# Two-layer cross-attention on one core: the blocks between a unit's five score runs dealt out anew, with a bank and an engine named for each

## The chip, the cores and the metric

The kernel runs on one core of a Trainium2 chip. The time is the device time of one launch in microseconds (us); smaller is better. The engines are TensorE (PE, with its weight loads as PEld), VectorE (DVE), ScalarE (ACT), GpSimd (POOL) and SyncE (SP), which here issues every DMA. Each engine works through its own list of instructions in order, and a semaphore wait at the head of a list holds everything behind it.

## The reference

Two layers of cross-attention over 32 sequences of 256 tokens (width 320, 20 heads of 16), each against 77 text rows of width 512. Cut to what matters, both layers are:

```python
q = heads(x @ Wq)                       # 20 heads of width 16
k, v = heads(text @ Wk), heads(text @ Wv)
p = softmax(q @ k^T / 4)                # over the 77 text rows
x = x + (merge(p @ v) @ Wo + bias)      # layer 1 reads layer 0's x
```

The further text parts of the reference (object, others, ip) have no rows for this input.

## The kernel before

The 8192 tokens are cut into 16 chunks of 512 (two sequences each); the two layers give 32 **units** u. Every fp32 product is made of rounded parts: a value's high part and what is left over (names ending in `S` hold both; `KH`/`KL`, `QH`/`QL`), with three products of high and low parts in place of one, 12 matrix instructions for a block of K or V (4 slices of the 512 inputs), 8 for a block of 128 outputs of Q or O, and 5 for the last 64 outputs.

Everything is written out by hand, engine by engine. One unit u on PE is:

- five **runs** `run(u, k, n)`: the scores of group k of unit u against the keys (24 products into the four banks of `pA`, then 16 more that subtract each row's maximum), and woven into them 8 products of unit n = u+1 in tokens-by-keys order, into two pairs of banks of `pR`. They serve only to find the maxima (`X` on DVE, a `tensor_reduce`). The first pair is written at the run's start (steps 0 and 1), the second at its end (steps 10 and 11).
- after each run ACT takes the exponential of all four banks of `pA` (`S`, the line of `ACT.Exp`); the next run writes `pA` and so waits for it (`take_four`). What PE does between two runs is called a **gap** here; a pair of an even and an odd unit has ten.
- in the gaps stand the other **blocks**: `K(w, m)` and `V(w, t)` of the next pair of units w (three each), `Q(u+2, m)` (three a unit), `PV(u, k)` (five a unit: probabilities times values, with the sums), `out(z, m)` of unit z = u-2 (three a unit, called O below), and `max_rows`, the transposition of the maxima, copied to `Mt` by ACT before the next unit's first run.

Every block takes one bank of `pR`, which is free again when DVE or ACT has read it. Before, the four banks go round in turn (`take`), and the reductions of the first pair of maxima free their two banks together.

From PV to O a unit goes a long way: DVE or ACT copy the five results to `Oraw` (`o_copy`); SP moves the sums to `Zg` and `Zt` (`sums`), DVE inverts them (`recip`), SP writes them to DRAM (`put_recips`) and reads them back spread over rows (`spread`, into `OS`); SP moves the rest of `Oraw` to `On` in 12 transfers (`natural`); POOL multiplies (`normalise`), ACT rounds and POOL and DVE take what is left over (`split_o`), then PE can run O. SP also loads the values into `VA` (`values`, three transfers a unit), stores the result of unit z (`store`) and loads X for unit u+3 (`load_x`) into one of five buffers, the one that unit z has just left. `split_x` on ACT and POOL makes the rounded parts of X.

Two of the waits that the text below speaks of, as the code has them before and after:

```python
if k == 0 and u:                       # o_copy, before it overwrites Oraw
    dve.wait_ge(d_on, 128 * u)         # all of natural(u-1, 0) and (u-1, 1) landed
    dve.wait_ge(d_zg, 32 * u)
...
if u >= XR:                            # load_x on SP
    sp.wait_ge(d_y[x], 32 * (u // XR)) # the store from this buffer landed
```

Of the kernel before, what the change touches and what calls it, by code (L numbers as in the profile page):

```python
# [47 lines left out]
def build(nc, a):  # L48
    with ExitStack() as ctx:
# [3 lines left out]
        def sem(name):  # L53
# [4 lines left out]
        Wk = sb("Wk", [128, 2, 4, KC], F32R)  # L58
# [10 lines left out]
        KH = sb("KH", [128, 3, 3, 2, LK], F32R)  # L69
        KL = sb("KL", [128, 3, 3, 2, LK], F32R)  # L70
# [13 lines left out]
        Zt = sb("Zt", [32, 64])  # L84
        stage = sb("stage", [128, 4, KC])
# [5 lines left out]
        ones = sb("ones", [L, 2, 2 * D])  # L91
# [9 lines left out]
        w_hi, x_hi, v_copied, q_hi0, q_hi1, q_hi2, q_half, mt_copied, p_done, o_hi = (  # L101
            sem(f"s_{n}") for n in (
                "w_hi", "x_hi", "v_copied", "q_hi0", "q_hi1", "q_hi2", "q_half", "mt_copied", "p_done", "o_hi"))

        w_lo, q_lo0, q_lo1, q_lo2, q_summed, x_max, r_done, r_last, o_tail, y_done, neg_done = (
            sem(f"s_{n}") for n in ("w_lo", "q_lo0", "q_lo1", "q_lo2", "q_summed", "x_max", "r_done", "r_last",
                                    "o_tail", "y_done",
                                    "neg_done"))
# [5 lines left out]
        o_raw = [sem(f"s_o_raw{k}") for k in range(NG)]  # L114
# [26 lines left out]
        VN = stage[:, :, :].rearrange("p k c -> p (k c)")[:, 0:4 * C].rearrange("p (t x) -> p t x", t=2)  # L141
        OL = stage[:, :, :].rearrange("p k c -> p (k c)").rearrange("p (m n) -> p m n", m=3)
        RL = C32[:, :, :].rearrange("p k n -> p (k n)")

        def k_parts(w):

            first = 2 * w % 3
            if first < 2:
                return [(slice(first, first + 2), slice(0, 4))]
            return [(slice(2, 3), slice(0, 2)), (slice(0, 1), slice(2, 4))]  # L150
# [11 lines left out]
        def _(pe):  # L162
            ring = [None] * NR
            turn = 0
            four = None

            def take(key, *readers):

                nonlocal turn
                b = turn % NR  # L170
# [228 lines left out]
            for m in range(3):  # L399
                K(0, m)  # L400
# [775 lines left out]
```

## Time and profile before

| what | us |
|---|---|
| three runs | 1049.4, 1052.84, 1042.22 (median 1049.4) |
| the profiled execution | 1039.82 |
| its span, first to last instruction | 1038.0 |
| PE / DVE / ACT / POOL busy | 936.3 / 638.4 / 553.8 / 385.5 |

The profiled execution lies 1.78 us above its span and 0.9% below the median of the three. Its sixteen pairs of units start at 43.31, 106.71, 170.49, 231.41, ..., 968.18 us; in between, most take 60.9 or 61.0 us, some 61.9 to 63.8. A pair starts with the first run of its even unit. In the timeline matrix instructions overlap, so what a block costs is read from its start to the start of what follows, not from its duration.

### The profile page before, as it was taken

What the parts mean: (1) busy time and instruction counts of PE and PEld (TensorE: products, weight loads), DVE (VectorE), ACT (ScalarE), POOL (GpSimd) and SP (SyncE); (2) the same over time, 40 slices, a digit from 0 to 9 for tenths busy, and PEclk for the clock granted to TensorE, in tenths of its full rate; (3) what the DMA queues carried; (4) which work ended last, traced back from release to release, by engine and by line L of the source; (5) the groups of instructions that cost most, each with busy time, mean ns of one, the idle gap of its engine ahead of it and who ended that gap; (6) DMA issues with size and microseconds to landing.
All of it is one profiled execution on the core that took longest, in us unless ns stands there. A gap on an engine that the chain in (4) does not pass through costs nothing.

```text
span 1038.0 us, 30058 instructions
## 1 busy us (share of the span) xinstructions
PE 936.3 (90%) x12848; PEld 741.2 (71%) x12848; DVE 638.4 (61%) x1007; ACT 553.8 (53%) x598; POOL 385.5 (37%) x208
## 2 busy tenths in 40 slices
PE   5799999999898999989999999999999999998987
PEld 5577767777676777777677777767777776876755
DVE  5554656666666566666656666665666656666636
ACT  4445545555555565556655654565554555555532
POOL 3403425334233523526453542533333252342023
PEclk9787989999999999999999999999999999999978
DMA  7203334443434364343535334353443434433232
GB/s 236 71 13 80 84 100 104 134 115 109 112 85 119 105 170 110 107 112 94 161 105 158 104 90 126 82 137 109 126 118 86 107 99 134 114 103 90 70 96 70
DMA packets 81491, 112.80 MB, mean 109 GB/s; under 512 B 22160, under 2 KB 38838, under 8 KB 81360
## 3 DMA queue, kind: packets, MB, share of 16 engines
q1 hardware_dynamic: 81360, 110.88, 39.3%
q8 instruction: 103, 1.69, 0.7%
q14 instruction: 28, 0.23, 0.1%
HBM read 60.50 MB, written 22.24 MB: 80 GB/s over the span
## 4 chain that ended last, share of the span: by engine, by line
PE 63%; DVE 22%; issue 6%; ACT 5%; DMA 2%; SPq 1%; POOL 1%; ACTq 0%; POOLq 0%; DVEq 0%
PE pR L239 29%; PE pR L212 9%; PE pR L226 9%; PE pR L348 8%; DVE Mx L720 7%; DVE X L786 4%; PE pA L293 4%; DVE KL L685 4%; PE pR L284 3%; DVE QL L694 2%; DMA OS<-rd 2%; PE pA L299 2%; ACT KH L507 2%; DVE Oraw L735 1%; DVE KH L679 1%
## 5 line engine op out<-in xcount | busy, mean ns | idle before, releaser
L566 ACT ACTIVATE P<-pA 77x2048 f32<-77x2048 f32 x160 | 300.2, 1876 | 261.1 <-PE pA L299 261.0
L720 DVE TENSOR_REDUCE Mx<-pR 128x8 f32<-128x616 f32 x320 | 247.4, 795 | 61.0 <-PE pR L284 60.2
L911 POOL TENSOR_TENSOR On<-On,OS 128x1024 f32<-128x1024 f32 (+1 forms) x62 | 112.7, 1837 | 340.0 <-DMA OS<-rd 340.0
L348 PE MATMUL pR<-P,VA 77*32 77x256 f32 x2480 | 165.6, 399 | 32.3 <-DVE Mx L720 32.0
L239 PE MATMUL pR<-XS,Wq 128*128 128x512 f32 x672 | 173.7, 402 | 2.6 <-DVE Mx L720 2.5
L284 PE MATMUL pR<-KH,QH 32*128 32x154 f32 x1280 | 141.8, 298 | 37.9 <-DVE Qt L702 15.6
L284 PEld LDWEIGHTS pR<-KH,QH 32*128 32x128 f32 x1280 | 102.0, 191 | 94.5 <-issue 72.9
L239 PE MATMUL pR<-OS,Wo 128*128 128x512 f32 x630 | 164.4, 409 | 4.9 <-DVE Mx L720 4.9
L293 PE MATMUL pA<-QH,KH 32*77 32x256 f32 x1280 | 150.1, 299 | 3.7 <-ACT Mt L556 3.6
L881 POOL TENSOR_TENSOR XS<-X,XS 128x1024 fp32r<-128x1024 f32 x32 | 76.4, 2386 | 197.6 <-ACT XS L495 197.6
L348 PEld LDWEIGHTS pR<-P,VA 77*32 77x32 f32 x2480 | 95.0, 142 | 76.3 <-issue 53.7
L239 PEld LDWEIGHTS pR<-OS,Wo 128*128 128x128 f32 x630 | 115.7, 191 | 44.7 <-issue 12.6
L239 PEld LDWEIGHTS pR<-XS,Wq 128*128 128x128 f32 x672 | 122.4, 190 | 30.7 <-DVE Mx L720 4.8
L293 PE MATMUL pA<-QL,KH 32*77 32x256 f32 x1280 | 140.0, 282 | 0.0
L293 PE MATMUL pA<-QH,KL 32*77 32x256 f32 x1280 | 139.9, 282 | 0.0
L735 DVE COPY Oraw<-pR 128x512 f32<-128x512 f32 x123 | 84.5, 687 | 40.9 <-PE pR L348 40.9
L212 PE MATMUL pR<-CS,Wk 128*128 128x308 f32 x576 | 95.8, 318 | 14.2 <-DVE Wk L661 10.6
L299 PE MATMUL pA<-Mt,neg 32*77 32x128 f32 x2560 | 106.8, 229 | 0.0
L694 DVE TENSOR_TENSOR QL<-pR,QH 128x512 fp32r<-128x512 f32 x64 | 44.2, 691 | 101.1 <-ACT QH L514 101.0
L786 DVE SCALAR_TENSOR_TENSOR X<-pR,bias,X 128x512 f32<-128x512 f32 (+1 forms) x93 | 69.3, 745 | 55.9 <-PE pR L239 55.9
L299 PEld LDWEIGHTS pA<-Mt,neg 32*77 32x77 f32 x2560 | 102.6, 147 | 0.0
L212 PEld LDWEIGHTS pR<-CS,Wk 128*128 128x128 f32 x576 | 87.3, 197 | 18.5 <-issue 15.9
(81 smaller groups left out, 1181.3 us busy)
## 6 DMA issues: line engine op xcount, KB each, us to landing
On<-Oraw SPq DMA_DIRECT2D x248, 64.0 KB
OS<-rd SPq DMA_DIRECT2D x62, 256.0 KB
C<-in_cT SPq DMA_DIRECT2D x16, 616.0 KB, 4.8
X<-in_xT SPq DMA_DIRECT2D x16, 512.0 KB, 3.9
y<-X SPq DMA_DIRECT2D x16, 512.0 KB, 4.0
X<-y SPq DMA_DIRECT2D x16, 512.0 KB, 3.9
out<-X SPq DMA_DIRECT2D x15, 512.0 KB, 4.0
X<-in_xT SPq DMA_DIRECT2D x32, 128.0 KB, 4.1
```

The costliest lines, as they stand in the source:

```text
L212: f = pe.matmul(p[:, 0:L4], Wk[:, s, k, 128 * m:128 * m + 128], CS[:, c, k, :], start=(k == 0 and s == 0 and c == 0), stop=(k == 3 and s = ...
L226: f = pe.matmul(out, CS[:, c, k, 128 * t:128 * t + M], Wv[:, s, k, :], start=(k == 0 and i == 0), stop=(k == 3 and i == 2))
L239: f = pe.matmul(p[:, :], W[:, k, c0:c0 + 128], S[:, s, :], start=(i == 0), stop=(i == len(pairs) - 1))
L284: return pe.matmul(pR[:, pair + j % 2, t * LK:t * LK + LK], QH[32 * j:32 * j + 32, n % 2, c0:c0 + 128], KH[32 * j:32 * j + 32, m, n % 3, b ...
L293: pe.matmul(pA[0:L, j, h * SQ:h * SQ + SQ], K_[32 * j:32 * j + 32, ms, u % 3, bs, pp * L:pp * L + L], Q_[32 * j:32 * j + 32, u % 2, c0:c0 ...
L299: return pe.matmul(pA[0:L, j, t * 128:t * 128 + 128], neg[32 * j:32 * j + 32, i:i + 1].broadcast_to([32, L]), Mt[32 * j:32 * j + 32, :], s ...
L348: f = pe.matmul(bank[32 * j:32 * j + 32, b * SQ:b * SQ + SQ], VA[0:L, u % 2, b, h:2 * C:H], src, start=True, stop=True, skip_group_check=True)
L566: act.activation(P[0:L, i % PR, :, :], pA[0:L, :, :], ACT.Exp, scale=float(D) ** -0.5).then_inc(p_done, 1)
L720: dve.tensor_reduce(Mx[:, :].rearrange("p (j i) -> p j i", j=4)[:, 2 * half:2 * half + 2, i:i + 4], pR[:, pair:pair + 2, 0:2 * LK].rearran ...
L735: dve.tensor_copy(Oraw[:, k, :], pR[:, slot["PV", u, k], :]).then_inc(o_raw[k], 1)
L786: dve.scalar_tensor_tensor(out=X32[0:M, x, m, :], in0=p[0:M, :], scalar=bias[0:M, l, m:m + 1], in1=X32[0:M, x, m, :], op0=ALU.add, op1=ALU ...
L911: pool.tensor_tensor(On[rows, blocks, :], On[rows, blocks, :], OS[rows, blocks, :].bitcast(F32), ALU.mult).then_inc(o_mul, 1)
```

## The change

- The bank is no longer taken in turn: each block's call names its bank, and each run names its first and second pair. In the prologue, and in the last unit, blocks also use the four banks of `pA`.
- The blocks of a pair of units are dealt over its ten gaps in a new order. DVE and ACT each get new lists: all copies of V are on DVE, eight of ten `o_copy` on ACT (before two), some roundings of Q and K on DVE (`Q_hi`, `K_hi`). SP's and POOL's lists are rewritten to fit.
- The maxima of a run's first pair of banks are two reductions, one for each bank (`X(n, k, part)`), each with its own semaphore; the second pair stays one reduction.
- The last block of K (64 outputs) takes 8 matrix instructions in place of 12: its 128 columns hold the high part's 64 and the left-over part's 64 side by side, and the two halves are added afterwards (`k_half_copy` on ACT, `k_sum` on DVE) into `Kt`. `KH2`/`KL2` hold this block, 2x77 wide for two sequences instead of 4x77.
- `Wk` is loaded 320 wide instead of 384.

The core of the diff:

```diff
-                p = take(("K", w, m), (k_lo[m], w + 1))
-                for k in range(4):
-                    for s, c in ((0, 0), (0, 1), (1, 0)):
+                if m == 2:
+                    p = take(("K", w, m), bank, (k_summed, w + 1))
+                    for k in range(4):
+                        pe.matmul(p[:, 0:L4], Wk[:, k, 256:384], CS[:, 0, k, :], start=(k == 0), stop=(k == 3), ...)
+                    for k in range(4):
+                        f = pe.matmul(p[0:64, 0:L4], Wk[:, k, 256:320], CS[:, 1, k, :], start=False, stop=(k == 3), ...)
...
+    # PE, one unit in full
+                if u % 2 == 0:
+                    run(u, 0, n, 2, 0)
+                    V(w, 2, 2)
+                    K(w, 1, 3)
+                    Q(u + 1, 1, 1)
+                    out(z, 1, 0)
+                    run(u, 1, n, 2, 0)
+                    out(z, 0, 3)
+                    V(w, 1, 1)
+                    run(u, 2, n, 2, 0)
+                    out(z, 2, 2)
+                    Q(u + 2, 2, 3)
+                    K(w, 2, 0)
+                    PV(u, 0, 1)
+                    run(u, 3, n, 2, 0)
+                    Q(u + 2, 0, 2)
+                    PV(u, 1, 3)
+                    run(u, 4, n, 0, 2)
+                    Q(u + 2, 1, 1)
+                    max_rows(n, 3)
+                    V(w, 0, 0)
+                    PV(u, 2, 3)
+                    PV(u, 4, 1)
+                    PV(u, 3, 0)
+                else:
+                    run(u, 0, n, 2, 0)
+                    out(z, 0, 2)
+                    run(u, 1, n, 0, 2)
+                    out(z, 1, 0)
+                    run(u, 2, n, 2, 0)
+                    PV(u, 0, 3)
+                    PV(u, 1, 0)
+                    run(u, 3, n, 2, 0)
+                    out(z, 2, 2)
+                    Q(u + 2, 2, 0)
+                    PV(u, 2, 1)
+                    run(u, 4, n, 2, 0)
+                    K(w + 1, 0, 2)
+                    max_rows(n, 1)
+                    Q(u + 2, 0, 3)
+                    PV(u, 4, 1)
+                    PV(u, 3, 0)
...
+    # ACT, even unit, behind its fifth run
+                    S(u, 4)
+                    max_rows(n)
+                    split_o(v, 0)
+                    split_x(u + 3)
+                    split_o(v, 1)
+                    o_copy(u, 4)
+                    o_copy(u, 3)
...
+    # SP, even unit
+                    sums(v, 2)
+                    values(u + 1)
+                    sums(v, 1)
+                    put_recips(v, 1)
+                    put_recips(v, 0)
+                    for r in range(3):
+                        natural(v, r)
+                    spread(v, 0)
+                    spread(v, 1)
+                    store(z)
+                    load_x(u + 3)
+                    load_c(u // 2 + 2)
+                    sums(u, 0)
...
+    # SP, odd unit
+                    sums(v, 2)
+                    sums(v, 1)
+                    if u < NU - 1:
+                        values(u + 1)
+                    natural(v, 0)
+                    put_recips(v, 0)
+                    put_recips(v, 1)
+                    natural(v, 1)
+                    natural(v, 2)
+                    spread(v, 0)
+                    spread(v, 1)
+                    store(z)
+                    if u < NU - 1:
+                        sums(u, 0)
+                    load_x(u + 3)
```

Here v = u-1, z = u-2 and w = u//2 + 1. Each place below is given as the engine's list has it, before and after.

PE, the first gap of an even unit, from the end of the run to the start of the next. Before (`L348` PV, `L239` O):

```order
L299 MATMUL pA<-Mt,neg 77x128 x2
L284 MATMUL pR<-KH,QH 128x154 x2
L348 MATMUL pR<-P,VA 32x256 x16
L239 MATMUL pR<-OS,Wo 128x512 x8
L284 MATMUL pR<-KH,QH 128x154 x2
```

Now (`L253` V, `L237` K, `L266` Q and O):

```order
L340 MATMUL pA<-Mt,neg 77x128 x2
L321 MATMUL pR<-KH,QH 128x154 x2
L253 MATMUL pR<-Wv,CS 52x320 x12
L237 MATMUL pR<-CS,Wk 128x308 x12
L266 MATMUL pR<-XS,Wq 128x512 x8
L266 MATMUL pR<-OS,Wo 128x512 x8
L321 MATMUL pR<-KH,QH 128x154 x2
```

Two PVs have moved to the end of the unit ahead; V, K, Q and another block of O stand here instead, 44 block products in place of 24.

SP, an odd unit, from the sums to the spread. Before (`L1013`, `L1018` the sums, `L1030` and `L1036` natural, `L1043`, `L1046` the inverted sums to DRAM, `L1060` spread):

```order
L1013 DMA Zg<-Oraw 64x1x64
L1018 DMA Zt<-Oraw 32x1x64
L1030 DMA On<-Oraw 16x2x512 x4
L1043 DMA rd<-Zg 128x64
L1046 DMA rd<-Zt 32x64
L1036 DMA On<-Oraw 16x512 x4
L1060 DMA OS<-rd 128x1x512 x2
```

Now (`small` holds what `Zt` held; `L1182` is `values`):

```order
L1200 DMA small<-Oraw 32x1x64
L1195 DMA Zg<-Oraw 64x1x64
L1182 DMA VA<-VS 77x320
L1182 DMA VA<-VS 51x320
L1182 DMA VA<-VS 26x320
L1212 DMA On<-Oraw 16x2x512 x4
L1226 DMA rd<-Zg 128x64
L1229 DMA rd<-small 32x64
L1212 DMA On<-Oraw 16x2x512 x4
L1219 DMA On<-Oraw 16x512 x4
L1243 DMA OS<-rd 128x1x512 x2
```

The first four natural transfers of a unit used to be issued ahead of this place, in the unit before; now they stand here, behind the three of the values.

DVE, an odd unit, from the inverted sums to the maxima of the fourth run. Before (`L741`, `L747` recip, `L786`, `L790` O, `L720` maxima, `L735` o_copy):

```order
L741 RECIPROCAL Zg<-Zg 128x64
L747 RECIPROCAL Zt<-Zt 32x64
L786 SCALAR_TENSOR_TENSOR X<-pR,bias,X 64x512
L790 TENSOR_TENSOR X<-pR,X 64x512
L786 SCALAR_TENSOR_TENSOR X<-pR,bias,X 128x512
L720 TENSOR_REDUCE Mx<-pR 128x2x4 x2
L735 COPY Oraw<-pR 128x512 x2
L720 TENSOR_REDUCE Mx<-pR 128x2x4 x2
```

Now (`L887`, `L893` recip, `L931` O, `L866` maxima, `L881` o_copy):

```order
L887 RECIPROCAL Zg<-Zg 128x64
L893 RECIPROCAL small<-small 32x64
L931 SCALAR_TENSOR_TENSOR X<-pR,bias,X 128x512
L866 TENSOR_REDUCE Mx<-pR 128x4 x2
L866 TENSOR_REDUCE Mx<-pR 128x2x4
L881 COPY Oraw<-pR 128x512
L866 TENSOR_REDUCE Mx<-pR 128x4 x2
L866 TENSOR_REDUCE Mx<-pR 128x2x4
```

One of the two o_copy has gone to ACT; the other, o_copy(u, 0), still stands between the maxima of runs 2 and 3, and waits for `d_on`.

## Rows read from the trace of the kernel before

**Rows 1.** Page, part 1: busy us, share of the span, instructions of each engine.

```profile
PE 936.3 (90%) x12848; PEld 741.2 (71%) x12848; DVE 638.4 (61%) x1007; ACT 553.8 (53%) x598; POOL 385.5 (37%) x208
```

**Rows 2.** Windows: stretch, length, busy us (count) PE PEld DVE ACT POOL, clock, DMA share, GB/s.

```profile
43.31:106.71 63.40, 54.49 (x725) 43.50 (x724) 32.19 (x58) 33.04 (x37) 13.23 (x7) 0.78 0.17 41
477.57:538.55 60.98, 56.34 (x800) 44.79 (x800) 38.56 (x60) 35.81 (x38) 28.80 (x15) 1.00 0.46 128
968.18:1038.00 69.82, 57.56 (x798) 41.41 (x797) 38.73 (x46) 25.83 (x24) 14.38 (x8) 0.85 0.30 84
```

**Rows 3.** Timeline of PE: start, duration, instruction, count, idle time before.

```profile
408.87 3.23 PE L239 MATMUL pR<-XS,Wq 128*128 128x512 f32 x13
...
411.96 3.73 PE L226 MATMUL pR<-Wv,CS 128*128 128x320 f32 x24
415.63 0.34 PE L284 MATMUL pR<-KH,QH 32*128 32x154 f32 x2
...
418.20 1.96 PE L348 MATMUL pR<-P,VA 77*32 77x256 f32 x32 [1.14 <-DVE Mx L720]
...
462.77 0.34 PE L284 MATMUL pR<-KH,QH 32*128 32x154 f32 x2
...
464.13 1.96 PE L212 MATMUL pR<-CS,Wk 128*128 128x308 f32 x12
465.93 2.00 PE L239 MATMUL pR<-XS,Wq 128*128 128x512 f32 x8
```

**Rows 4.** Waits: who waited for whom, total us, times, longest.

```profile
PE pR L348 <- DVE Mx L720: 32.0, 42, 1.1
```

**Rows 5.** DVE by shape: line, names, shapes, count, busy us, mean ns, idle before.

```profile
L720 DVE TENSOR_REDUCE Mx<-pR 128x8 f32<-128x616 f32 x320 | 247.4, 795 | 61.0 <-PE pR L284 60.2
...
L685 DVE SCALAR_TENSOR_TENSOR KL<-pR,mask,KH 128x308 fp32r<-128x308 f32 x66 | 32.5, 534 | 31.8 <-ACT KH L507 31.3
...
L685 DVE SCALAR_TENSOR_TENSOR KL<-pR,mask,KH 128x154 fp32r<-128x154 f32 x60 | 18.5, 371 | 19.9 <-ACT KH L507 19.7
```

**Rows 6.** Timeline of ACT behind the run that starts at 415.63.

```profile
417.09 1.87 ACT L566 ACTIVATE P<-pA 77x2048 f32<-77x2048 f32 x1 [0.62 <-PE pA L299]
```

**Rows 7.** ACT by shape: rounding X, and one copy of a result (columns as in rows 5).

```profile
L495 ACT ACTIVATE XS<-X 128x1536 fp32r<-128x1536 f32 x32 | 47.2, 1476 | 1.1 <-DMA X<-in_xT 1.1
...
L574 ACT ACTIVATE Oraw<-pR 128x512 f32<-128x512 f32 x32 | 19.0, 597 | 26.1 <-PE pR L348 26.1
```

**Rows 8.** Timeline of SP: start and duration of the issue (not of the transfer).

```profile
420.13 0.63 SPq L1013 DMA_DIRECT2D Zg<-Oraw  x1
...
421.64 2.64 SPq L1030 DMA_DIRECT2D On<-Oraw  x4
424.96 0.34 SPq L1043 DMA_DIRECT2D rd<-Zg  x1
...
428.39 1.91 SPq L1060 DMA_DIRECT2D OS<-rd  x3
...
430.83 0.53 SPq L1071 DMA_DIRECT2D y<-X  x1
437.52 0.38 SPq L970 DMA_DIRECT2D X<-in_xT  x1
437.94 1.14 SPq L972 DMA_DIRECT2D X<-in_xT  x2
439.18 2.48 SPq L1000 DMA_DIRECT2D VA<-VS  x3
```

**Rows 9.** Timeline of POOL: the product released by the spread issued at 428.39.

```profile
434.14 3.64 POOL L911 TENSOR_TENSOR On<-On,OS 128x1024 f32<-128x1024 f32 x2 [9.97 <-DMA OS<-rd]
```

**Rows 10.** DMA issues, KB each, median us from issue to landing.

```profile
On<-Oraw SPq DMA_DIRECT2D x124, 32.0 KB, 1.9
...
y<-X SPq DMA_DIRECT2D x16, 128.0 KB, 6.5
```

**Rows 11.** Line 972 (X for a later unit), issue to landing.

```profile
DMA to landing us min/median/max: 3.7/4.0/8.2
```

More of the change, by code:

```diff
@@ L196, in take_four @@
                     pe.wait_ge(four[0], four[1])
+                else:
+                    for b in range(NR, 2 * NR):
+                        for reader in ring[b] or ():
+                            pe.wait_ge(*reader)
                 four = (freed, value)
+                for b in range(NR, 2 * NR):
+                    ring[b] = (four,)
             def weights(name, l):
@@ L401, in _ @@
-            for m in range(3):
-                Q(0, m)
-            for t in range(3):
-                V(0, t)
-            for k in range(NG):
-                run(None, k, 0)
-            Q(1, 0)
-            max_rows(0)
-            Q(1, 1)
-            Q(1, 2)
+                pe.wait_ge(o_tail, u + 1)
+                pe.wait_ge(o_lo, u + 1)
+                p = take(("O", u, m), bank, freed)
+                project(p, Wo, OS, m).then_inc(o_pe, 1)
+            K(0, 0, 4)
+            K(0, 1, 5)
@@ L650, in _ @@
+            for k in range(NG):
+                S(NU - 1, k)
+            split_o(NU - 2, 0)
+            split_o(NU - 2, 1)
             for m in range(3):
@@ L847, in _ @@
-            o_copy(v, 4)
+                    maxima(n, 0, 0, 1, 2)
+                    recip_last(v)
+                    recip(v)
+                    split_o(z)
+                    K_lo(w, 1)
+                    V(w, 2)
+                    Q_lo(u + 1, 1)
+                    out(z, 1)
+                    maxima(n, 1, 1, 0, 2)
+                    out(z, 0)
+                    V(w, 1)
+                    maxima(n, 2, 0, 1, 2)
+                    out(z, 2)
+                    q_sum(u + 2)
@@ new lines, in _ @@
+                    k_sum(w)
+                    maxima(n, 3, 0, 1)
+                    K_hi(w, 2)
+                    maxima(n, 3, 2)
+                    K_lo(w, 2)
+                    Q_lo(u + 2, 0)
+                    maxima(n, 4, 1, 0, 2)
+                    Q_hi(u + 2, 2)
+                    Q_lo(u + 2, 2)
+                    Q_hi(u + 2, 1)
+                    Q_lo(u + 2, 1)
+                    V(w, 0)
+                    o_copy(u, 2)
+                    split_o(v)
+                else:
+                    maxima(n, 0, 0, 1, 2)
+                    out(z, 0)
+                    maxima(n, 1, 0, 1, 2)
+                    recip(v)
+                    recip_last(v)
+                    out(z, 1)
+                    maxima(n, 2, 1, 0, 2)
+                    o_copy(u, 0)
+                    maxima(n, 3, 0, 1, 2)
+                    out(z, 2)
+                    q_sum(u + 2)
+                    maxima(n, 4, 0, 1, 2)
+                    Q_hi(u + 2, 2)
+                    Q_lo(u + 2, 2)
+                    K_hi(w + 1, 0)
+                    K_lo(w + 1, 0)
+                    Q_lo(u + 2, 0)
@@ L848, in _ @@
+            u, v, z = NU - 1, NU - 2, NU - 3
             out(z, 0)
+            out(z, 1)
             recip(v)
@@ L984, in values @@
                 w, half = u // 2, u % 2
-                sp.wait_ge(v_copied, 3 * w + 2 + half)
+                for t in (half, half + 1):
+                    sp.wait_ge(v_copied[t], w + 1)
                 if u == NU - 1:
```

850 lines of the change are left out of this document (445 added, 405 removed).

## The prediction

> **What bounds the kernel now.** I read the busy times first: PE is busy 90% of the span, no other engine above 61% [rows 1]. Then the windows: a pair of units in the middle takes 60.98 us at full clock, the first pair 63.40 at 0.78, though it has no O blocks, the end 69.82 at 0.85 [rows 2]. So the kernel is sixteen equal laps, and a lap is worth reading block by block on PE's timeline [rows 3]. A run is 1.36 us to its successor (462.77 to 464.13), a K block 1.80 (464.13 to 465.93), 13 products of Q 3.09 (408.87 to 411.96), two V 3.67 (411.96 to 415.63), two PVs 1.96. A lap of ten runs (13.6), three K (5.4), three V (5.5), 42 products of Q and 42 of O (84 at 0.24 = 20.2), ten PVs (9.6) and two transpositions (0.2) comes to 54.5. The other 6.4 us of 60.9 are waits of PE, mostly for a bank: 1.14 before a PV, until DVE has reduced the run's last maxima; in all 32.0 us in 42 such waits [rows 3, 4].
>
> **The change part by part.** *K's third block:* four products fewer a lap, each 1.80/12 = 0.15: -0.6 a lap, -9.6 in all 16, all on PE's path. What it adds (a copy on ACT, sums on DVE) has a gap to hide in.
>
> *The new deal.* A bank is named so that the first block of a gap goes to one whose maxima are long reduced. In the even unit I find no block that needs the bank of the second pair before DVE is through with it, so the 6.4 us can go. But a gap has a floor: the exponential starts 1.46 us behind the run's start and takes 1.87 [rows 3, 6], so runs are at least 3.4 apart. In the odd unit the gaps 0 to 2 hold one O, one O and two PVs, 1.8 to 2.0 us, just at that floor: +0.5 a lap with the last maxima before PV(u, 1). The even unit is then five runs, 6.8, and gaps of 7.4, 3.9, 4.5, 2.9 and 6.8 = 32.3 us by the blocks above, the odd, from run to run, 3.4, 3.4, 3.5, 4.8, 7.2 = 22.3: a lap of 54.6 (54.5-0.6+0.5 says the same within 0.2).
>
> *The split maxima.* 308 elements are not in the trace as a reduction. The products of K with 154 and 308 elements take 371 and 534 ns, 1.06 ns an element, so half of the 795 ns reduction is 795-326 = 469, and two are 0.14 us more than one [rows 5]: 160 times, 23 us of DVE work. Bounds: 0 (nothing but the elements) and 0.4 each (no saving by size). With eight copies on ACT, DVE's 38.6 us in a lap [rows 2] become about 40; the extra hides behind PE, except where DVE's list is held.
>
> *SP's list: where the gain is given back.* An issue costs SP time: a sum 0.63, four natural 2.64, an inverse 0.34, three values 2.48, the spread 1.91, X 1.52 [rows 8]. And load_x(u+3) waits until store(z) has landed, 6.5 us behind its issue [rows 10]: 430.83 to 437.52 SP does nothing [rows 8]. The replay, from an even unit's start:
> - SP comes out of the last load_x at +1.2. Sums 2 to 1.8, values to 4.4, sums 1 to 5.0, landed about 6.3 (1.9 from issue, as a natural transfer [rows 10]). recip stands on DVE ahead of split_o(z), so that ends near 7.6, and O(z, 1), due at 6.9, starts at 7.7: **+0.8**.
> - O(z, 2) ends at 17.6; spread must wait for it: 17.7 to 19.6; the second store at 20.1, landed 26.6; X issued to 28.1, landed 31.5 (4.0 [rows 11]). ACT stands before split_x(u+3) from 30.0 on: 1.5 for it, then about 0.6 for split_o's small half and twice 0.6 for the copies [rows 7], 34.9. The next unit starts at 33.3 and needs the second copy's bank at its eleventh step of twelve, 34.4: **+0.5**.
> - Odd unit, from its start: o_copy(v, 3) done 1.7, sums to 2.4, values to 4.9, natural(v, 0) to 7.5, both inverses to 8.3, natural(v, 1) to 10.9, landed 12.2. DVE's o_copy(u, 0) waits for that landing, and run 3 waits for its bank: 12.9 in place of 10.6: **+2.3**. Behind the waiting copy on DVE stand the maxima of run 3; PE has nothing in between.
> - O(z, 2) ends 15.7, spread to 17.6, store landed 24.6, X issued to 26.1; the unit ends at 25.0, which gives the +1.2 above back: the lap closes on itself.
>
> A lap: 54.6+0.8+0.5+2.3 = 58.2. The spread has room: POOL starts 5.75 behind its issue and needs 3.64 [rows 8, 9], done at 27.1 and 25.4 where ACT comes at 29 and 25.7.
>
> On this the Trainium skill speaks otherwise: "DMA: Bandwidth & Descriptors", section "Issuing engines are not separate DMA queues", calls the sequencer's time to initiate a DMA "usually small relative to the DMA itself". By it the three waits would shrink to the first two rivals' side. Rows 8 show 0.6 of issue against 1.9 of landing for a natural transfer, so here the issues count.
>
> *Prologue.* K(1, 0) is added to it and Q(1, 1) leaves it; run 0 now also waits for K(1, 0)'s left-over on DVE, since that block sits in a bank of `pA`. DVE gets that block's four 0.53 us operations and five split maxima [rows 5]. I take the first run at 45.1, 1.8 later than 43.31 [rows 2] (bounds -3 and +4: the V blocks between the maxima may win more).
>
> *First lap.* No O and no store wait: about 51.3 at full clock. Before, the same sum is 60.9-10.2 = 50.7 and it took 63.40 with the granted clock at 0.78 [rows 2], so the slow clock cost 12.7. Here gaps are as empty; I take 9.7 (bounds 0 and 13): 61.0. The Trainium skill, "TensorE: Matmul & The Clock Gate", section "What's actually happening", says that the throttled state is the default and activity releases it; a busier first lap would then come to the lower end, 51.3.
>
> *End.* The last unit's new list uses `pA` banks, but split_o(30) on DVE now stands behind three divisions; against that ACT copies the maxima earlier in its list. The laps' two SP waits stand there too. 68 in place of 69.8 (bounds 61 and 72).
>
> **Sum.** 45.1 + 61.0 + 14 x (58.2 + 0.5) + 68 = 996; the 0.5 is what the laps before average above 60.9. With 1.8 around the span, 998 against 1039.8; the median is 0.9% above that execution, so **1007 us**, -4%.
>
> **The rivals.**
> - *A, the deal works as dealt.* The three SP waits don't bite (earlier issues or quicker transfers): laps of 54.6+0.5, first lap 57, end 63: 45+57+771+63+2 = 938, times 1.009 = **946**. For it: every term of 54.6 is a measured block. Against: the issues are measured too. In between, with the +2.3 alone gone, 970.
> - *B, only K's products count.* The waits move and don't go, since DVE's list has an operation in every gap that PE needs: 1049.4-9.6 = **1040**. DVE at 40 of 58 us makes it possible, the named banks speak against it.
> - *C, slower.* X for unit u+3 is now needed right after it lands, in the even unit. If it lands like the slowest, 8.2 us instead of 4.0 [rows 11], each lap is 4.2 longer: 62.4, in all 1055 times 1.009 = **1064**. It decides from 2.7 us a lap on. Against it: the median is 4.0, and DMA is busy under half of the time [rows 2].
>
> **Chances.** A change of 1% is about what can be told. Forecast 0.72 (own range 962 to 1035), A 0.13, B 0.07, C 0.06, rest 0.02. Faster by over 1% (below 1038.9) takes the forecast and A: 0.86; same 0.08; slower 0.06. The range reaches into A and to B, 946 to 1040, and leaves out C and A's lower half.
>
> **What would show it.** Laps of 58.2, the longest PE wait in an odd unit before run 3, released by `Oraw` on DVE, itself held by the landing of `On`; a wait before O(z, 1) in the even unit; ACT idle for X before split_x; no waits of PV for `Mx`. A is right if laps are 55 and PE idles only 0.1 before runs. I am wrong if `Mx` still ends PE's waits, or if the clock falls inside the middle laps.

## The result: 1075.2 us, 2.6% slower, and the profile after

The change makes the kernel slower: 1075.24 us (median of 1072.38, 1073.21, 1077.26 and 1080.05) against 1049.12 on the same chip, a ratio of 1.026 with a 95% interval of 1.019 to 1.033. The prediction said 1007, 946 to 1040. The profiled execution took 1072.38 with a span of 1070.6, so some 1.8 us around the span are as before.

The page of the kernel after, parts 1 and 4 (busy time, and the chain that ended last by engine and line):

```profile
PE 946.5 (88%) x12784; PEld 745.4 (70%) x12784; DVE 652.6 (61%) x1190; ACT 554.4 (52%) x564; POOL 389.5 (36%) x209
...
PE 53%; DMA 20%; SPq 12%; issue 7%; DVE 5%; ACT 3%; DVEq 0%; ACTq 0%
PE pR L266 22%; PE pR L387 7%; DMA out<-X 7%; PE pA L334 7%; DMA y<-X 6%; PE pR L321 6%; DMA Zg<-Oraw 5%; PE pR L253 4%; SPq L1243 4%; SPq L1182 3%; PE pA L340 3%; SPq L1153 2%; PE pA L266 1%; ACT Oraw L659 1%; DVE Mx L866 1%
```

Nearly a third of the chain is now transfers and SP's issues: the store (`out<-X`, `y<-X`), the sums (`Zg<-Oraw`), the spread (`L1243`), the values (`L1182`), the loads of X (`L1153`). PE has 64 instructions fewer than in [rows 1] (four for each of sixteen K blocks) and is busy for 10 us more: some of its instructions ran at the lower clock (the granted clock is 0.94 in the mean, before 0.97).

Windows of the first lap, one in the middle, and the end (columns as in rows 2):

```profile
45.13:108.71 63.58, 56.72 (x752) 44.32 (x752) 31.05 (x62) 30.58 (x29) 14.83 (x8) 0.76 0.17 39
745.92:809.34 63.42, 58.00 (x798) 46.02 (x794) 39.78 (x74) 33.91 (x34) 23.33 (x13) 0.95 0.41 108
996.95:1070.60 73.65, 56.07 (x777) 40.92 (x773) 40.43 (x48) 28.69 (x26) 18.86 (x11) 0.88 0.31 80
```

A lap in the middle is 63.4 us where it was 60.98 at full clock [rows 2]. From the starts of the even units on PE's timeline, the fourteen middle laps are 63.45 us in the mean against 61.53 before. That is where the loss comes from: first run +1.8, first lap +0.2, 14 laps x 1.92 = +26.9, end +3.8; in all 32.7 us, which are, but for rounding, the 32.6 between the two profiled executions.

The waits of PE and of those that it waits for (waiter <- releaser: us in total, times, longest):

```profile
PE pR L321 <- DVE Oraw L881: 46.4, 15, 4.4
...
ACT Oraw L659 <- DMA On<-Oraw: 37.7, 14, 3.8
...
DVE Zg L887 <- DMA Zg<-Oraw: 19.4, 15, 2.4
PE pR L266 <- DVE OS L922: 19.3, 13, 2.6
...
ACT XS L549 <- DMA X<-y: 16.5, 8, 2.7
...
PE pR L266 <- DVE Mx L866: 10.6, 11, 1.7
```

The 32.0 us in which PV waited for `Mx` [rows 4] are gone: for PV the named banks do what they were named for. In their place stand, thirteen to fifteen times each, a wait of up to 4.4 us for `o_copy` and one for `split_o`. ACT waits for X in both layers, 16.5 us in eight laps of the second and 13.1 us in seven of the first. Waits for `Mx` remain before blocks of Q and O, 10.6 us in 11; nine of them stand before O(z, 0) of an odd unit, and a fence below shows why.

The lap that starts at 745.92, on PE's timeline (columns as in rows 3):

```profile
754.32 2.11 PE L266 MATMUL pR<-OS,Wo 128*128 128x512 f32 x8 [1.54 <-DVE OS L922]
...
765.28 0.73 PE L226 MATMUL pR<-CS,Wk 128*128 128x308 f32 x4
765.85 0.72 PE L229 MATMUL pR<-CS,Wk 128*64 128x308 f32 x4
766.50 1.10 PE L387 MATMUL pR<-P,VA 77*32 77x256 f32 x16
...
781.64 0.34 PE L321 MATMUL pR<-KH,QH 32*128 32x154 f32 x2 [0.25 <-ACT Oraw L659]
...
788.84 2.19 PE L387 MATMUL pR<-P,VA 77*32 77x256 f32 x32
794.67 0.49 PE L321 MATMUL pR<-KH,QH 32*128 32x154 f32 x2 [3.63 <-DVE Oraw L881]
```

In order: O(z, 1) of the even unit waits for `split_o`; the 8-product block of K takes 1.22 us (765.28 to 766.50); the odd unit's run 0 is held at its last steps; run 3 of the odd unit waits 3.6 us for the bank that `o_copy(u, 0)` reads. The releasers, on DVE and on ACT, first DVE:

```profile
751.08 0.55 DVE L893 RECIPROCAL small<-small 32x64 f32<-32x64 f32 x1 [2.78 <-DMA small<-Oraw]
752.99 0.55 DVE L887 RECIPROCAL Zg<-Zg 128x64 f32<-128x64 f32 x1 [1.37 <-DMA Zg<-Oraw]
753.58 0.68 DVE L922 TENSOR_TENSOR OS<-On,OS 64x512 fp32r<-64x512 f32 x1
...
793.83 0.69 DVE L881 COPY Oraw<-pR 128x512 f32<-128x512 f32 x1 [4.04 <-issue]
```

```profile
778.62 1.49 ACT L549 ACTIVATE XS<-X 128x1536 fp32r<-128x1536 f32 x1 [1.77 <-DMA X<-y]
780.01 0.62 ACT L667 ACTIVATE OS<-On 64x512 fp32r<-64x512 f32 x1
780.53 1.06 ACT L659 ACTIVATE Oraw<-pR 128x512 f32<-128x512 f32 x2
```

In another lap, of the first layer, the same late rounding holds PE a second time. DVE's `split_o` waits for ACT's rounding of O, which stands behind `split_x`; the maxima of run 0 stand behind `split_o` on DVE, and O(z, 0) needs the bank that they free:

```profile
458.17 1.97 DVE L922 TENSOR_TENSOR OS<-On,OS 64x512 fp32r<-64x512 f32 x1 [1.79 <-ACT OS L667]
460.17 1.57 DVE L866 TENSOR_REDUCE Mx<-pR 128x4 f32<-128x308 f32 x3
```

```profile
460.80 2.08 PE L266 MATMUL pR<-OS,Wo 128*128 128x512 f32 x8 [1.20 <-DVE Mx L866]
```

And SP's issues in the lap that starts at 745.92 (start and duration of the issue):

```profile
746.30 1.14 SPq L1153 DMA_DIRECT2D X<-y  x2
747.54 0.61 SPq L1200 DMA_DIRECT2D small<-Oraw  x1
748.26 2.67 SPq L1182 DMA_DIRECT2D VA<-VS  x3
751.04 0.61 SPq L1195 DMA_DIRECT2D Zg<-Oraw  x1
...
764.38 1.89 SPq L1243 DMA_DIRECT2D OS<-rd  x3
766.39 0.39 SPq L1254 DMA_DIRECT2D out<-X  x1
766.82 0.56 SPq L1255 DMA_DIRECT2D out<-X  x1
773.55 0.38 SPq L1151 DMA_DIRECT2D X<-y  x1
...
781.83 0.79 SPq L1195 DMA_DIRECT2D Zg<-Oraw  x1
782.72 2.52 SPq L1182 DMA_DIRECT2D VA<-VS  x3
785.36 2.71 SPq L1212 DMA_DIRECT2D On<-Oraw  x4
788.11 0.59 SPq L1226 DMA_DIRECT2D rd<-Zg  x1
...
789.28 2.71 SPq L1212 DMA_DIRECT2D On<-Oraw  x4
```

Read against the fences of the same lap: the sums issued at 751.04, behind the values, let `recip` start at 752.99, `split_o` at 753.58 and O(z, 1) at 754.32. X is issued from 773.55, when the store of 766.82 has landed, and ACT can round it at 778.62; PE's run 0 has been going since 780.03. The fourth transfer of natural(v, 1) is issued by 791.99, and DVE's copy, whose wait for `d_on` the profile only calls "issue", starts at 793.83.

**The lap in four stretches.** For the experiments I read a lap from O(z, 2) of one unit on. Every number is a difference of two starts on PE's timeline, the median over the thirteen laps of units 4 to 29. Rows are kernels of the experiments below; the first row is what PE needs when it hardly waits.

| kernel | A: odd O(z, 2) to even O(z, 1) | B: to even O(z, 2) | C: to the odd unit's run 1 | D: to odd O(z, 2) | sum |
|---|---|---|---|---|---|
| all three moves (e4) | 17.35 | 8.47 | 20.58 | 8.29 | 54.7 |
| after | 20.06 | 8.59 | 22.22 | 12.63 | 63.5 |
| e1, SP's odd list | 19.49 | 8.62 | 22.39 | 8.54 | 59.0 |
| e2, SP's even list | 18.37 | 8.47 | 21.94 | 12.79 | 61.6 |
| e3, split_x later | 20.24 | 8.59 | 20.58 | 12.66 | 62.1 |
| e10, e1 with e3 | 20.18 | 10.10 | 20.58 | 8.28 | 59.1 |

### The profile page after: what moved, and what is told of

The parts are those of the page before. It is cut to its first block, busy times and chain, and to the rows that moved or that the text cites. A ratio compares the mean times of both kernels' runs of the same rounds, so it can differ in the third digit from the quotient of the medians.

```text
span 1070.6 us, 30568 instructions
## 1 busy us (share of the span) xinstructions
PE 946.5 (88%) x12784; PEld 745.4 (70%) x12784; DVE 652.6 (61%) x1190; ACT 554.4 (52%) x564; POOL 389.5 (36%) x209
## 4 chain that ended last, share of the span: by engine, by line
PE 53%; DMA 20%; SPq 12%; issue 7%; DVE 5%; ACT 3%; DVEq 0%; ACTq 0%
PE pR L266 22%; PE pR L387 7%; DMA out<-X 7%; PE pA L334 7%; DMA y<-X 6%; PE pR L321 6%; DMA Zg<-Oraw 5%; PE pR L253 4%; SPq L1243 4%; SPq L1182 3%; PE pA L340 3%; SPq L1153 2%; PE pA L266 1%; ACT Oraw L659 1%; DVE Mx L866 1%
## 5 line engine op out<-in xcount | busy, mean ns | idle before, releaser
L866 DVE TENSOR_REDUCE Mx<-pR 128x4 f32<-128x308 f32 (+1 forms) x480 | 260.2, 580 | 70.3 <-PE pR L321 63.0
L266 PE MATMUL pR<-OS,Wo 128*128 128x512 f32 x638 | 187.7, 437 | 29.2 <-DVE OS L922 19.3
L266 PE MATMUL pR<-XS,Wq 128*128 128x512 f32 x638 | 172.0, 410 | 2.2 <-DVE Mx L866 2.1
L266 PEld LDWEIGHTS pR<-OS,Wo 128*128 128x128 f32 x638 | 123.6, 206 | 65.2 <-DVE OS L922 34.5
L334 PE MATMUL pA<-QH,KL 32*77 32x256 f32 x1280 | 144.8, 288 | 0.0
L266 PEld LDWEIGHTS pR<-XS,Wq 128*128 128x128 f32 x638 | 120.6, 196 | 29.6 <-issue 2.6
L931 DVE SCALAR_TENSOR_TENSOR X<-pR,bias,X 128x512 f32<-128x512 f32 (+1 forms) x93 | 69.6, 748 | 84.5 <-PE pR L266 83.0
L340 PE MATMUL pA<-Mt,neg 32*77 32x128 f32 x2560 | 113.8, 235 | 0.0
L659 ACT ACTIVATE Oraw<-pR 128x512 f32<-128x512 f32 x124 | 72.2, 593 | 79.4 <-PE pR L387 41.2
L340 PEld LDWEIGHTS pA<-Mt,neg 32*77 32x77 f32 x2560 | 108.2, 153 | 0.0
L334 PEld LDWEIGHTS pA<-QL,KH 32*77 32x77 f32 x1280 | 97.2, 151 | 0.0
L334 PEld LDWEIGHTS pA<-QH,KL 32*77 32x77 f32 x1280 | 97.1, 151 | 0.0
L1092 POOL TENSOR_TENSOR OS<-On,OS 128x1024 fp32r<-128x1024 f32 x31 | 74.2, 2392 | 59.0 <-ACT OS L667 59.0
```

The source lines that it names most:

```text
L266: f = pe.matmul(p[:, :], W[:, k, c0:c0 + 128], S[:, s, :], start=(i == 0), stop=(i == len(pairs) - 1))
L334: pe.matmul(pA[0:L, j, h * SQ:h * SQ + SQ], kt[:, pp * L:pp * L + L], Q_[32 * j:32 * j + 32, u % 2, c0:c0 + SQ], start=(i == 0), stop=Fals ...
L340: return pe.matmul(pA[0:L, j, t * 128:t * 128 + 128], neg[32 * j:32 * j + 32, i:i + 1].broadcast_to([32, L]), Mt[32 * j:32 * j + 32, :], s ...
L659: act.activation(Oraw[:, k, :], psum(slot["PV", u, k])[:, :], ACT.Copy).then_inc(o_raw[k][u % 2], 1)
L866: dve.tensor_reduce(Mx[:, :].rearrange("p (j i) -> p j i", j=4)[:, j:j + banks, i:i + 4], pR[:, bank:bank + banks, 0:2 * LK].rearrange("p ...
L931: dve.scalar_tensor_tensor(out=X32[0:M, x, m, :], in0=p[0:M, :], scalar=bias[0:M, l, m:m + 1], in1=X32[0:M, x, m, :], op0=ALU.add, op1=ALU ...
```

## The experiments

Each is the kernel after with one edit, except where it says otherwise. The kernel before ran beside each group of them, at 1044.2, 1042.6 and 1046.4 us; ratios are against it.

**e1: SP's odd list.** The two natural transfers for which `d_on` counts go ahead of the inverses and the values:

```diff
                     sums(v, 2)
                     sums(v, 1)
-                    if u < NU - 1:
-                        values(u + 1)
                     natural(v, 0)
+                    natural(v, 1)
                     put_recips(v, 0)
                     put_recips(v, 1)
-                    natural(v, 1)
                     natural(v, 2)
+                    if u < NU - 1:
+                        values(u + 1)
                     spread(v, 0)
```

> One edit in the changed kernel: in the odd unit SP issues the values behind the natural transfers, and the first eight natural transfers ahead of the inverted sums. Theory (SP's list holds DVE's o_copy(u, 0) until natural(v, 1) has landed, PE waits about 3.6 us before run 3, and the clock falls to half in that wait): the eight transfers are issued 3.3 us earlier, the wait before run 3 falls under 0.5 us, the three blocks behind it run at full clock again (2.8 us), a lap goes from 63.4 to 57 to 58 us, the time from 1075 to 980 to 1000 us. Rival (DVE's list is too full in the odd unit, the next operation is as late): run 3 gets at most 1 us earlier, 1050 to 1075 us.

Measured: 1018.15 us, 0.977 [0.970, 0.985]. Stretch D falls from 12.63 to 8.54, so the wait of run 3 is SP's order. The time misses the 980 to 1000 that were expected: laps are 59.8 in the mean, since stretches A and C keep their 2.1 and 1.8 us above e4's. Of PE's waits in e1:

```profile
PE pR L266 <- DVE OS L922: 30.6, 14, 5.0
```

The wait for `split_o` has grown from 19.3 to 30.6 us. What stood before it is shorter: stretch A is a chain (spread, store, its landing, X, sums, recip, split_o) of about 20 us, and PE's own work in it (e4's A) only fills 17.35.

**e2: SP's even list.** Both sums go ahead of the values, and X for the coming even unit is loaded behind the sums instead of ahead of them, at the end of the odd unit:

```diff
                     sums(v, 2)
-                    values(u + 1)
                     sums(v, 1)
+                    if u:
+                        load_x(u + 2)
+                    values(u + 1)
...
-                    load_x(u + 3)                  # odd unit
```

> One edit in the changed kernel: SP issues both sums ahead of the load of X and the values at the even unit's start (the load leaves the odd unit's end, where SP stood until the store had landed). Theory: the inverted sums come 4 us earlier, the wait of PE before O(z, 1) of the even unit, 1.45 us a lap, goes, and nothing else: lap 62.0, 1050 to 1058 us. Rival (O(z, 1) waits for another part of the chain, the rounding on ACT or POOL): no change, 1070 to 1080 us.

Measured: 1051.46 us, 1.007 [1.003, 1.011], within the 1050 to 1058 expected. Stretch A falls from 20.06 to 18.37 and O(z, 1) no longer waits; the other two stay.

**e3: split_x behind the exponential of the odd unit's run 0.** On ACT alone:

```diff
                     max_rows(n)
                     split_o(v, 0)
-                    split_x(u + 3)
                     split_o(v, 1)
...
                     S(u, 0)                        # odd unit
+                    split_x(u + 2)
```

> One edit in the changed kernel: ACT rounds X of unit u+3 behind the odd unit's first exponential instead of ahead of the last two copies of the even unit. Theory: the copies no longer wait for X to land, run 0 of the odd unit loses its 1.6 us wait, the sums and natural transfers start 1.4 us earlier, so run 3 comes 1.4 us earlier too: lap 60 to 61, 1020 to 1040 us. Rival (the copies are late for another reason, or the exponential behind pays for the rounding): 1065 to 1080 us.

Measured: 1059.45 us, 1.015 [1.010, 1.020]; a miss by 20 us. Run 0 is back at 1.37 us and stretch C at 20.58, 1.64 shorter, but A and D are no shorter than before the edit. The theory behind my number, that the one wait feeds the others, is wrong. A and C each begin at an O(z, 2), behind which SP issues the spread and its chain starts afresh; what leads to run 3 came earlier together with run 0, and D stayed. The edit also takes the waits for `Mx` before O(z, 0): of 10.6 us in 11 waits before Q and O, 2.1 us in two are left. So C held two waits that one late rounding made.

**e4: the three moves together.**

> The three edits of the other runs together. Theory: all three waits go and with them the half clock in the laps: laps of 55 to 56 us, 940 to 965 us, faster than the kernel before by 8 to 10%. Rival (the deal of blocks itself costs, through DVE's list of 40 us a lap): laps stay at 59 or above, over 1010 us.

Measured: 947.65 us (943.9 to 949.33), 0.907 [0.902, 0.912], 9.3% below the kernel before. This is the time of rival A (946) with its laps of 55. The chain that ended last, and a lap of e4 by windows:

```profile
PE 86%; DVE 4%; SPq 3%; ACT 2%; DMA 2%; issue 2%; POOL 1%; POOLq 0%; ACTq 0%; DVEq 0%
```

```profile
489.31:544.06 54.75, 54.75 (x801) 43.59 (x798) 38.97 (x74) 35.04 (x36) 24.79 (x13) 1.00 0.50 130
```

PE is busy for all of the 54.75 us. SP's issues around a change of laps, to hold against those of the kernel after:

```profile
543.95 0.57 SPq L1200 DMA_DIRECT2D small<-Oraw  x1
544.85 0.54 SPq L1195 DMA_DIRECT2D Zg<-Oraw  x1
545.49 0.40 SPq L1151 DMA_DIRECT2D X<-y  x1
```

The lap starts at 544.06: the second sums are issued 0.8 us behind it, where they were 5.1 behind it (751.04 - 745.92). No issue is left out, and an issue costs about what it did: a transfer of natural(v, 0) or (v, 1) takes 0.59 us (median) in both kernels.

**e10: e1's and e3's moves without e2's.**

> The kernel after with two of the three moves, SyncE's odd list and ScalarE's split of X, without the one on SyncE's even list. Theory (each wait is paid by itself, and the loop feeds one into the next): only the wait ahead of O(z,1) is left, 1.5 to 4 us a lap, laps of 56.5 to 59 and a time of 965 to 1010 us. If the waits simply add, the laps are 55.0 + 1.5 = 56.5 and the time 970. Rival: with both odd waits gone the sums' transfer is early enough by itself, and the time is e4's, some 948.

Measured: 1005.1 us, 0.960 [0.955, 0.965], in the upper part of the expected 965 to 1010. C and D are e4's; A stands at 20.18:

```profile
PE pR L266 <- DVE OS L922: 42.8, 14, 5.0
```

42.8 us over 14 laps are 3.1 a lap; another 1.6 lies in stretch B, where O(z, 1) itself takes 3.56 in place of 1.90 us at the lower clock behind the long wait. So the move that brought 1.9 us a lap alone (e2: 63.5 to 61.6 in the table's sum) brings 4.4 where it is the last one missing (59.1 to 54.7).

**e5: the clock.** In the kernel after, the granted clock falls in the wait ahead of run 3. Windows around the wait (the wait, and what follows it):

```profile
788.80:793.80 5.00, 2.23 (x37) 1.23 (x32) 0.99 (x2) 1.88 (x1) 0.26 (x1) 1.00 0.50 84
793.80:800.60 6.80, 5.93 (x56) 5.14 (x57) 3.28 (x6) 2.47 (x2) 0.00 (x0) 0.50 0.06 14
```

The first is at 2.4 GHz with PE busy for 2.23 of 5.00 us, the second at 1.2 GHz: run 3 takes 2.44 us, O(z, 2) 2.30 (1.37 and 1.27 in e4). To see whether this sets the lap, the products of PV(u, 1) in odd units are issued four times (the result is only that of the last pass), so that PE is busy while it waits:

```diff
-                    PV(u, 1, 0)
+                    PV(u, 1, 0, times=4)
...
-                for b in range(2):
+                for b in [0, 1] * times:
```

> The changed kernel with more work: in the odd unit the 16 products of PV(u, 1) are issued four times over (the same result is written again), just where PE waits about 3.4 us before run 3; 48 products more, 2.9 us of PE work a lap. Theory (the clock falls because PE stands still there, and run 3, O(z, 2) and Q behind it then run at half clock, some 2.3 us a lap): these blocks take 1.37, 1.26 and 1.25 again, laps go from 63.4 to about 61, the time from 1075 to 1040 to 1050 us, though the kernel does more. Rival (the clock falls in the laps for another reason, or costs nothing): 1070 to 1085 us.

Measured: 1081.26 us, 1.036 [1.029, 1.042], where 1040 to 1050 was expected; this is the rival's range. Run 3, O(z, 2) and Q(u+2, 2) are back at 1.37, 1.27 and 1.25 us, and the low clock in the middle laps falls from 81.9 to 41.0 us in all. Yet a lap is 63.5 in the mean (its median is 62.7 for 63.6; two laps take 68.5, each with a wait of 5.0 us for `split_o`). What the clock gives back, waits take again: from run 1 to run 3 of the odd unit it is 10.54 for 10.19, C is 22.50 for 22.22, and PE waits for `split_o` 29.0 us in all for 19.3. How much of the first is the added products' own time is not separated. So the lower clock follows the wait; without it a median lap is 0.9 us shorter, and the time no shorter.

**e6 and e12: K's third block with 12 products again, on e4.** The four products more are the block's first four issued again (`for k in [0, 1, 2, 3] * 2`); the second pass starts its sums anew (`start=(k == 0)`), so the result is the same.

> The version with all three edits (947.7 us), with 12 products again in K's third block: its first four are issued twice, the second time over the first. Theory: 0.6 us a lap on PE's path, since the laps have nothing left that hides it: 9 to 10 us more, 957. Rival (the block stands in a gap with slack): 948.

> The same kernel as e6. The four products of K's third block cost 0.57 us a lap and once more in the prologue, some 9 us in all. If the excess of e6 over that (it stood 19 us above e4) was a granted clock that fell at another point of the start-up, this run may stand anywhere from 9 to 19 us above its neighbour e11; if the products themselves cause it, it is 17 to 21 us again, with a first run at 47.7 us or later.

Measured: 966.64 us, 0.926 [0.921, 0.930], and 968.36, 0.924 [0.920, 0.928], against 947.65 for e4 and 951.84 for the same kernel beside e12 (e11, for which 944 to 950 was expected). For e6 957 was expected, so it is missed by 10 us; e12 stands 16.5 us above its neighbour with a first run at 46.17, which is the first of its two cases and not the 17 to 21 with a first run at 47.7. The block takes 1.79 for 1.22 us, +0.57 as expected. But the middle laps are 56.3 in both runs against 55.3 and 55.4. In e12 the run of PE behind which Q(u+2, 1) stands takes 1.90 in the mean for 1.48, its median unchanged: in a few laps DVE's left-over of Q is late. The waits of PE in e12:

```profile
PE pR L321 <- DVE QL L832: 4.7, 5, 1.1
```

The first lap of e12 is 3.5 longer than that of its neighbour, with 27.3 us at the lower clock against 21.8. The four products are thus worth 16 to 19 us here, 9 of them on PE and the others through lateness and clock. How these split was not settled.

**e7: the first pair's maxima as one reduction, on e4.** As in the kernel before, with one semaphore for both banks:

```diff
-                for part in range(3):
+                for part in (0, 2):
...
-                j, banks = (2, 2) if part == 2 else (part, 1)
+                j, banks = part, 2
```

> The version with all three edits (947.7 us), with the first pair of maxima in one reduction of 616 again, both banks freed by it. Theory: the first block of a gap wants its bank 1.37 us behind the run's start, the one reduction is through at 1.3 to 1.7 where DVE comes to it late: 0 to 0.3 us for most of ten gaps, 950 to 975 us. Rival (DVE gains 0.08 us an operation and PE loses nothing): 943 to 948 us.

Measured: 963.36 us, 0.924 [0.920, 0.927], where e4 has 0.907 and, as e11, 0.910: laps of 56.1 in place of 55.3 in the mean; 950 to 975 was expected. PE waits for `Mx` 32 times for 10.6 us in front of blocks of Q and O, and 13 times for 3.6 us in front of a PV. In e4 it waits for `Mx` before Q and O twice, 2.1 us, and before PV never.

**e8: the split maxima alone, in the kernel before.**

```diff
-                for half in range(2):
+                for j, banks in ((0, 1), (1, 1), (2, 2)):
...
-                        pair = take_pair((x_max, 2 * (NG * n + k) + 1))
+                        pair = take_pair(((x_max, 3 * (NG * n + k) + 1), (x_max, 3 * (NG * n + k) + 2)))
```

> The kernel before with one part of the change: the maxima of a run's first pair in two reductions, each freeing its bank. Theory: in six or seven of its ten gaps PE waits for the bank of the first pair, and gets it 0.3 us earlier: 1.5 to 2.2 us a lap, 1015 to 1030 us against 1049. Rival (the extra DVE time moves other waits): 1045 to 1060 us.

Measured: 1019.09 us, 0.978 [0.974, 0.982], within the 1015 to 1030 expected. Laps have a median of 59.22 against 60.97 (mean 60.3 against 61.5). The reduction of one bank, in e8:

```profile
L721 DVE TENSOR_REDUCE Mx<-pR 128x4 f32<-128x308 f32 x320 | 137.3, 470 | 45.1 <-PE pR L284 44.5
L721 DVE TENSOR_REDUCE Mx<-pR 128x8 f32<-128x616 f32 x160 | 126.9, 793 | 11.4 <-PE pR L284 7.6
```

Two of 470 ns are 0.15 us more DVE work than one of 793, and bring 1.75 us in a median lap: the first bank is free some 0.3 us earlier (793 - 470 ns), and PE's waits for `Mx` before PV, Q, O and K fall from 43.0 us in all to 19.8. This one edit of the change gives 2.2% by itself, and the rest of it takes that back and more.

**e9: both ends, on e4.** ACT rounds V's first weights before Q's first block, and DVE takes the last `split_o` before the last division:

```diff
                     k_half_copy(0)
+                    weight_hi("Wv", 0)             # ACT, prologue; it stood behind q_half_copy(0)
...
                     divide_last(1)
+                    split_o(v)                     # DVE, the last unit
                     divide_last(2)
-                    split_o(v)
```

> The kernel with all three moves (e4), with two more at its ends: ScalarE prepares V's first weight block right behind K's halves, ahead of Q's first block, and VectorE takes the last unit's split of O ahead of the last division instead of behind it. Theory: both ends hold waits of TensorE that only this order makes. The first run starts at about 42 us in place of 45.3 (a wait of 3.5 us of TensorE ahead of V's first block goes), and the tail, 72.9 us with all three moves, falls by about 2: 4 to 6 us less than e4 on the same chip. Rival: VectorE or ScalarE is late next at either end, or the granted clock takes it back, and the time is within 1.5 us of e4's.

> The same kernel as e4, as the reference on this chip: 944 to 950 us and a first run at 45.3 us.

Measured: 943.98 us, 0.903 [0.898, 0.907], with e4's kernel on the same chip at 951.84, 0.910 [0.907, 0.914]. The start is as expected: the first run begins at 41.48 and not 45.05. The end isn't. Its wait of PE in e9, and under it DVE's timeline there:

```profile
934.41 5.91 PE L266 MATMUL pA<-OS,Wo 128*128 128x512 f32 x13 [6.31 <-DVE OS L922]
```

```profile
932.20 2.16 DVE L922 TENSOR_TENSOR OS<-On,OS 64x512 fp32r<-64x512 f32 x1 [2.08 <-ACT OS L667]
934.38 1.76 DVE L909 RECIPROCAL C<-pA 128x256 f32<-128x256 f32 x1
```

PE waits 6.31 us where it waited 6.03: `split_o` has been moved ahead of the division and now waits 2.08 us for ACT instead. The profiled spans differ by 2.0 us, the medians by 7.9, where 4 to 6 was expected; only the 3.6 us of the start are traced to their cause. e9 is the best version that was run, 9.7% below the kernel before.

## Why the prediction was wrong, step by step

**The sum against the trace.** Predicted span 996, measured 1070.6:

| term | predicted | measured |
|---|---|---|
| first run starts | 45.1 | 45.13 |
| first lap | 61.0 | 63.58 |
| 14 laps | 14 x 58.7 | 14 x 63.45 |
| last pair and end | 68 | 73.6 |

66.5 of the 74.6 us missed are in the laps.

**The floor, 54.6: right.** e4's laps have a median of 54.99 and its four stretches sum to 54.7. The gap where the exponential sets the pace, K's 8 products and all blocks cost what [rows 3, 6] said. K's block saves 0.57 of the 0.6. (The first gap of an even unit holds 40 block products, V 12, K 12, Q 8 and O 8, and not the 44 given above; the sum took it right, as 7.4 us.)

**The split maxima, +0.14 us of DVE work each: right in the cost, silent on the gain.** 472 ns in the kernel after for an estimated 469. What a bank free earlier brings, 1.75 us in a median lap of the kernel before (e8), was hidden in the 6.4 us that "can go" by the named banks; by e7 the banks alone would not have done it, since 0.9 us a lap then comes back.

**The three SP waits: the mechanism right, the sizes the step that failed.** The list in "SP's list: where the gain is given back" names the three places, their waiters and their releasers, and the trace and e1 to e4 bear them out: with three moves on SP and ACT, and no work taken away, the laps fall to the floor. The sum was 54.6 + 0.8 + 0.5 + 2.3; its last three terms are what failed. Their sizes, read as the median of the block that holds the wait against its length in e4:

| wait | predicted | measured |
|---|---|---|
| O(z, 1), even | 0.8 | 1.4 (Q and its wait, 3.26 for 1.84) |
| run 0, odd | 0.5 | 1.6 (3.01 for 1.37) |
| run 3, odd | 2.3 | 3.4 (4.44 for 1.03) |
| lower clock behind it | none | 2.4 (run 3, O(z, 2), Q(u+2, 2): 6.28 for 3.89) |

That is some 8.8 where I had 3.6; 54.7 and 8.8 are the 63.5 of the laps.

The case of run 3, replayed from the odd unit's start (780.03) with the fences above: sums issued to 2.6 (predicted 2.4), values to 5.2 (4.9), natural(v, 0) to 8.0 (7.5), inverses to 9.1 (8.3), natural(v, 1) to 12.0 (10.9), the landing 13.8 (12.2), run 3 at 14.6 (12.9). From the end of the sums to the end of natural(v, 1) SP took 9.4 us where the durations of [rows 8] had given 8.5: the issues themselves are a little longer (the two inverses took 1.1 for 0.8), and some 0.1 us stands between two groups. And the transfer landed later. The 1.9 us of [rows 10] are those of the 32 KB transfers of natural(v, 2); the wait is for the 64 KB ones, whose landing no row of before gives. The kernel after has both:

```profile
On<-Oraw SPq DMA_DIRECT2D x248, 64.0 KB, 2.4
...
On<-Oraw SPq DMA_DIRECT2D x124, 32.0 KB, 2.0
```

So the replay read its landing from the wrong row. The even unit's case slips in the same way: second sums issued at 5.1 (predicted 4.4), `Zg` ready at 7.1 (6.3), O(z, 1) at 8.4 (7.7). For run 0 the trace has 7.1 us in 13 waits for ACT's copy, about the 0.5 predicted; what the list did not have is the second waiter, `split_o` on DVE with the maxima behind it, nine waits of 0.4 to 1.7 us, and e3 removes both. These are small errors in one entry and large in the sum, because the replay was a chain with no slack in it, and I gave the term no upper bound: the range ended at rival B, not at what the replay would give with dearer issues.

The page on DMA that the prediction weighed against the rows (the Trainium skill, "DMA: Bandwidth & Descriptors", "Issuing engines are not separate DMA queues") would have had the waits shrink. The rows and e4 decide against that here: an issue of 0.59 us stands against a landing of 1.9 to 2.4, and the same issues in another order on SP, with one move on ACT, are worth some 12% of the time.

**The lower clock in the middle laps: missing.** I named it in the last sentence as what would make me wrong, and priced it at nothing. The kernel before already showed what the clock does when PE has little to do [rows 2]; a forecast wait of 2.3 us in every lap should have been given a clock term with a bound. By e5 it isn't what sets the lap: with run 3, O(z, 2) and Q back at full clock, waits take back all but 0.9 of the 2.4 us, so the term doesn't simply add to the others. The other sign named there, waits that `Mx` ends, is seen too, 10.6 us; by e3 they follow from the late rounding of X and not from the banks.

**First run: right by luck.** 45.13 for 45.1, though PE waits 3.0 us before V's first block for ACT (e9), which the sum did not have.

**First lap, +2.6.** The full-clock value, 51.3, holds: e4 and e11 are one kernel and took 55.67 and 59.71 us with 11.7 and 21.8 us at the lower clock, 0.40 us for each, which leads back to 51.0. What missed is the share of time at the lower clock: 30.7 us, so 12.3 us lost, and I took 9.7. "TensorE: Matmul & The Clock Gate" (the Trainium skill, "What's actually happening") says that the throttled state is the default and that activity releases it; from that I took that a busier lap would come to 51.3. The kernel after doesn't bear this out: its first lap has 30.7 us at the lower clock, where that of the kernel before, 63.40 us at 0.78 [rows 2], had some 27.

**End, +5.6.** `split_o(30)` on DVE, named as a risk, makes PE wait 6.5 us ahead of the last O blocks, and the O(z, 1) wait stands there with 2.07. I set a gain against them that isn't there: e4's end is 72.9. In e9 ACT turned out to be late next.

**The rivals.** C had the right sign with the wrong mechanism: X's landing has a median of 4.2 and not 8.2, and no run shows it as the whole loss. A came true in e4 only. B's reason, a DVE list that holds PE in each gap, isn't seen. Two of the rivals' sums are a little off by their own terms: "in between" comes to 974 and not 970, C to 1066 and not 1064; neither decides anything. The right rival for "slower" was my own forecast with its three waits one and a half to three times as large.

## What to carry to other kernels

- When an order written by hand is dealt anew, the queue that issues the transfers has to be dealt with it, by deadline: who waits for each landing, and when. Here the values, needed much later, stood in front of the transfers that two engines waited for.
- Cut a lap at the points where its long chain starts afresh, and hold each stretch against the chain's latency. Here a stretch was about the larger of PE's work and the chain; what is saved elsewhere in a stretch only makes its last wait longer, so moves can be worth little one by one (1 to 5% here) and 12% together.
- A replay with no slack needs an upper bound. Here SP's issues took 9.4 us for 8.5, so add some 10% to every issue, take the landing of a transfer of the same size, look for every engine that waits behind the same landing, and let the range reach there. Give the clock a term where a forecast wait comes back in every lap.

## What the runs showed of the hardware

- A transfer issued right behind larger ones was ready late. The first sums of the even unit (`small`), issued at 747.54 behind three transfers of X, let DVE's recip start at 751.08, 3.5 us later; the second (`Zg`), issued at 751.04, did at 752.99, 1.95 us later. In thirteen laps of the kernel after the first took 2.5 to 4.2 us, the second 1.94 to 1.98. That the transfers of X are the cause is likely, but not shown: the two also differ in size and shape, and with X behind them (e2, e4) DVE hardly waited for either, so that their landing isn't seen.
- Behind PE's wait of 3.6 us before run 3, with PE busy for 2.2 of 5.0 us, the granted clock stood at 1.2 in place of 2.4 GHz for 6.8 us. Over the fourteen middle laps it stood there for 81.9 us. In e10, behind waits of up to 5.0 us, O(z, 1) took 3.56 us for 1.90.
- One kernel on two chips (e4, e11) spent 11.7 and 21.8 us of its first lap at the lower clock, with nothing changed in the program. The laps differ by 4.0 us (55.67 and 59.71), so a first lap is read with that much doubt.
- A reduction of 308 elements took 472 ns and one of 616 took 796: some 0.15 us for each instruction and 1.05 ns for each element.
